# A state-space stage on one core: the loop of three turns of two groups becomes straight code on all five engines

## What is computed

```python
xz = einsum('bld,ed->ble', rmsnorm(layernorm(x)), in_proj_w); xi, z = split(xz, 2)
u = silu(conv4(xi) + conv_b)                      # 512 channels
dt, Bm, Cm = split(einsum('bld,ed->ble', u, x_proj_w))
delta = softplus(dt @ dt_proj_w.T + dt_proj_b)
def step(h, inp):                                 # one step for each of 1024 positions
    delta_t, B_t, C_t, u_t = inp
    h = exp(delta_t[..., None] * A) * h + (delta_t * u_t)[..., None] * B_t[:, None, :]
    return (h, einsum('bds,bs->bd', h, C_t))      # 16 states for each channel
y = (ys + u * D_param) * silu(z)
x = x + (x + y @ out_proj_w.T)                    # the block's input is layernorm(x)
```

## Time and profile before

| | |
|---|---|
| median of 3 runs | 3620.05 us (3619.46 to 3624.98) |
| the profiled execution's own time | 3639.42 us |
| its span, first to last instruction | 3637.7 us |
| this stage's scans, first to end (8 groups) | 65.1 to about 1030 us |
| the looped groups 1 to 6 | 184.6 to 914.6 us |
| busy over the span | PE 85%, DVE 68%, ACT 46%, POOL 44% |

### The profile page before, as it was taken

One profiled execution on the slowest core, in us unless ns is written; L12 is line 12 of the kernel. 1 busy time (PEld: TensorE's weight loads), 2 busy tenths in 40 slices (PEclk: granted clock), 3 DMA queues, 4 the chain that ended last, 5 costly groups with the idle time before them and its releaser, 6 DMA issues. The chain is left out here.

```text
span 3637.7 us, 53305 instructions
## 1 busy us (share of the span) xinstructions
PE 3093.1 (85%) x15700; PEld 1825.8 (50%) x15701; DVE 2460.9 (68%) x4639; ACT 1662.0 (46%) x3131; POOL 1618.1 (44%) x1645
## 2 busy tenths in 40 slices
PE   6898899889779799897988998976978787997795
PEld 3343334333258544445444486643654575664474
DVE  6999899999976585766858565973348672224245
ACT  5767666667445355574655653321223231223031
POOL 4998889889855312212131263115443000001643
PEclk9999999999999889898998999988999898998898
DMA  4555455556510000000000004501345791000246
GB/s 142 146 140 143 131 142 141 132 140 145 145 35 1 16 2 2 1 2 2 2 2 2 1 1 123 143 1 70 119 131 161 155 110 30 12 12 0 87 131 211
DMA packets 358189, 282.73 MB, mean 78 GB/s; under 512 B 214124, under 2 KB 274320, under 8 KB 357940
## 3 DMA queue, kind: packets, MB, share of 16 engines
q1 hardware_dynamic: 344884, 246.16, 26.8%
q0 software_dynamic: 13056, 33.65, 2.7%
HBM read 205.41 MB, written 76.16 MB: 77 GB/s over the span
## 5 line engine op out<-in xcount | busy, mean ns | idle before, releaser
L709 POOL TENSOR_TENSOR mamba_dBu<-mamba_du,mamba_bcs 128x512 f32<-128x512 f32 x512 | 639.5, 1272 | 95.4 <-DMA mamba_bcs<-mamba_bc 74.4
L628 PE MATMUL mamba_banks<-mamba_hc,ident 128*128 128x512 f32 x1024 | 529.7, 629 | 111.2 <-DVE mamba_hc L947 110.7
L873 ACT ACTIVATE mamba_banks<-mamba_delta,mamba_a_neg 128x512 f32<-128x512 f32 x512 | 351.9, 690 | 178.0 <-DVE mamba_hc L947 166.5
L1749 DVE TENSOR_REDUCE attn_mp<-attn_banks 128x1 f32<-128x512 f32 (+2 forms) x576 | 356.3, 679 | 49.5 <-PE attn_banks L1440 43.2
L628 PEld LDWEIGHTS mamba_banks<-mamba_hc,ident 128*128 128x128 f32 x1024 | 179.1, 194 | 418.2 <-DVE mamba_hc L947 302.6
L947 DVE TENSOR_TENSOR mamba_hc<-mamba_banks,mamba_bcs 128x512 f32<-128x512 f32 x512 | 343.1, 671 | 9.0 <-PE mamba_banks L628 9.0
L940 DVE TENSOR_TENSOR_SCAN mamba_banks<-mamba_banks,mamba_h_end,mamba_dBu 128x512 f32<-128x512 f32 x256 | 326.6, 1276 | 17.5 <-ACT mamba_banks L873 9.3
L940 DVE TENSOR_TENSOR_SCAN mamba_banks<-mamba_banks,mamba_dBu 128x512 f32<-128x512 f32 x256 | 312.1, 1219 | 36.1 <-POOL mamba_dBu L709 19.4
L1437 PE MATMUL attn_banks<-attn_kT,attn_qT 96*128 96x512 bf16 (+3 forms) x768 | 252.4, 363 | 9.5 <-ACT attn_kT L1631 5.3
L1451 PE MATMUL attn_banks<-attn_qT,attn_kT 98*128 98x512 bf16 (+3 forms) x768 | 210.2, 328 | 8.8 <-ACT attn_r L1649 4.0
L1116 POOL TENSOR_TENSOR ffn_hs<-ffn_h,ffn_hs 128x512 fp32r<-128x512 f32 x128 | 162.1, 1296 | 97.3 <-ACT ffn_hs L1145 97.3
(11 more groups left out here) (422 smaller groups left out, 6608.2 us busy)
## 6 DMA issues: line engine op xcount, KB each, us to landing
mamba_bcs<-mamba_bc SPq DMA_DIRECT2D x256, 512.0 KB, 5.0
moe_slots_moe<-moe_pad SPq DMA_DIRECT2D x2, 9252.0 KB, 53.2
moe_xg<-moe_slots_moe SPq DMA_DIRECT2D x144, 128.5 KB
mix_qkv<-mixA_qkv SPq DMA_DIRECT2D x8, 1536.0 KB, 5.9
mixA_y<-moe_rows SPq DMA_DIRECT2D x16, 512.0 KB, 6.0
mix_qk<-mix_qkv SPq DMA_DIRECT2D x16, 512.0 KB, 7.4
mix_v<-mix_qkv SPq DMA_DIRECT2D x16, 256.0 KB, 7.6
mix_out<-mixB_oh SPq DMA_DIRECT2D x16, 256.0 KB, 7.5
```

Source lines behind the costliest of these rows:

```text
L628: pe.matmul(banks[:, SUMS + k % PAIR, :], c.ident[:, :], hc[:, n % RING, :], start=False, stop=True, skip_group_check=True).then_inc(sem(" ...
L709: pool.tensor_tensor(dBu[:, n % RING, :], du[:, v, k, :], bcs[:, i_of(n) % 4, 0, :], ALU.mult)\
L873: act.activation(banks[:, n % RING, :], delta[:, v, k, :], ACT.Exp, scale=a_neg[:, k, st:st + 1])\
L1749: dve.tensor_reduce(dst, src, AX.X, ALU.max).then_inc(sem("ring_used"), 1)
```

## The change

```diff
--- before.py
+++ after.py
@@ -517,7 +517,7 @@
         def group_loop(engine, group):

             group(0, 0, False, True)
-            with engine.Fori(0, B - 1) as m:
+            for m in range(B - 1):
                 group(m * 2 + 1, 1, True, True)
                 group(m * 2 + 2, 0, True, True)
             group(G - 1, 1, True, False)
```

## The result

| | before | after |
|---|---|---|
| median of 5 runs | 3620.05 us (3614.08 to 3624.98) | 3596.57 us (3592.84 to 3600.58) |
| ratio | | 0.9939, 95% interval 0.9927 to 0.9951 |

The account below looks back on a forecast made before the run. The state-space stage was taken to run at DVE's pace, with fetch stalls at loop returns. Gains of 8.36 and 4.19 made 12.55 us, other terms zero, taking the 3620.05 median to 3607.5; range 3599 to 3615 (8 in 10).

Parts of the forecast that it names:

- The two returns on DVE: State-space loop: DVE's idle of 4.51 and 3.70 us at its two returns goes, worth 8.36 us by group lengths.
- Rival 2: State-space seams: stall only in the profiled execution, or POOL, ACT or a transfer late; gain 0 to 6 us, chance 0.12.
- What the stall leaves behind: Groups 3 and 5: PE's long idle, low clock and DVE's ninth-tile wait go, making them like group 1; 4.19 us.
- Rival 1: State-space stage: only the stall goes, the ninth tile's wait stays; gain 8.4 us, time 3611.7, chance 0.12.
- Sequencer arithmetic and the fetch of straight code: State-space stage: small loop instructions hidden by DVE's work, and fetching straight code hidden too; both costed at nothing.
- Rival 3: State-space groups on DVE: fetch of straight code isn't hidden, making the kernel slower; 3651 us, chance 0.05.
- What stands behind the stage: Later loops, attention's first: code moves, stalls stay but may change length; value 0, with 5 us either way.
- Rival 4: Attention's returns or a later loop get shorter by the move, 5 us and more on top; 3601, chance 0.08.
- The base: Whole kernel: the same 12.5 us come off the 3620.05 median as off the profiled 3639.42 us.

Follow-up runs that it names:

- e2: Kernel before with only DVE's state-space loop written straight, plus 45 semaphore increments holding DVE's later code in place: 3629.66 us, ratio 0.9969.
- e3: Kernel before with the state-space loop written straight on PE, ACT, POOL and SP, DVE keeping its loop: 3640.08 us, ratio 0.9991.
- the third measurement: The changed kernel, unaltered, timed a third time beside the kernel before on another chip: 3596.91 us, ratio 0.9952.
- e16: Kernel before with only DVE's state-space loop straight and 45 semaphore increments, repeated on a chip where before takes 3617.05: 3602.01 us, ratio 0.9962.
- e8: Changed kernel with attention's loop on DVE also written straight: 3624.55 us, ratio 0.9953 to before; the changed kernel took 3622.39 on that chip.

## Why the prediction came out as it did

**The two returns on DVE (8.36 us): right.** The idle ahead of the first scans is gone, e2 and e3 show that it was DVE's own code, and that POOL, which the trace names, was not what it waited for. Rival 2 fell with it: the stalls stood in every trace with DVE's loop, and the timed runs kept the gain.

**What the stall leaves behind (4.19 us): right.** PE's long idle, its stretch at the lower clock and the long wait at the ninth tile went together, and e3 shows them stay together. Groups 3 and 5 came out at 120.00 and 120.31, with 120.28 named. Rival 1 is refuted. The two terms are 12.55 us; the pair of traces has 13.2, all traces together 13.6, and the timed runs with DVE's part alone have 12.5. By a control-flow cost of 108 ns alone (the Trainium skill, Advanced Engine Details and Errata, section Control Flow Timing) this would have been next to nothing (0.2 us). The branch in the row does take 63 ns, and the time is behind it.

**Sequencer arithmetic and the fetch of straight code (0): right.** Busy times and group 7 are unchanged, and no "issue" wait appeared in the stage. Rival 3 fell for this reason.

**What stands behind the stage (value taken 0, 5 either way): here the prediction failed.** It named the place, attention's returns on DVE, and that the head's place in its packet decides. It then took zero, said that these stalls stay, and priced the gain that they might bring by how much longer they were than the first stage's second return (1.3 us for both), with 5 us either way beside it. What it missed is that such a wait comes in whole packets, as the experiments show. A wait of 4.2 us was two fetches, and the shift took one of them off each return, 2.3 and 2.5 us of waiting; the place of this code measured 4.6 us of the kernel's time on average instead of 0. The place of the head could have been counted in the built programs of before and after, 63 and 18 of 128, and the 8 KB of a packet stood in the earlier trace rows. Counting would not by itself have told which offset has the second fetch, but it would have shown that the offset changes by 45 of 128. With about 4.6 us for it the forecast would have been 3602.9, nearer to the result, which would still lie 6 us lower.

**The rest, 3 to 5 us.** 22.1 measured less 12.5 and 4.6 leaves 5; against the average of 20.6 over the three measurements it is 3.5. Of this 1.3 may be the other engines' code, which was costed at nothing. What remains isn't placed, and is within the scatter of one comparison. That the result fell 2.4 us below the range is therefore in part chance: a gain of 17.4 us, as the third measurement had, would have been 3602.7 here, inside it. Rival 4, "more than forecast", with 3601, was the case; its 0.08 was too low.

**The base.** That the same 12.5 us come off the median as off the slower profiled execution held: e2 and e16, on a chip where before takes 3641 us and on one where it takes 3617, have 11.3 and 13.7.

## What to carry to other kernels

A hardware loop can cost a fetch at each return: here DVE's loops of 756 and 529 instructions waited 1.8 to 5.1 us there, and the feed-forward's of 126 instructions went on within 0.3 us. On the engine that sets the pace the wait also leaves the others idle, and here PE's clock fell behind it; look for idle time ahead of the first instruction of a turn and compare it with the same passage where no return stands. In this stage only the engine that sets the pace needed its code straight: that one program brought 12.5 us, the other four together 1.3 on average, which can't be told from nothing. When an edit changes a program's length, list every loop behind it that waits at its return and work out where its head moves within a packet; and take two chips, and a repetition, before you believe a gain of 5 us in 3600.

## What was unexpected of the hardware

- DVE's code comes in packets of 8 KB that hold 128 instructions (39 packets for 4848 recorded instructions of four engines). Forty instructions of shift put the second wait between two particular statistics (1.53 and 1.68 us), 45 put it back ahead of the first instruction (4.40 and 4.46 in one), 128 changed nothing (4.29 and 4.24).
- The same wait costs unequally. Of 4.2 us at a return of attention, the first 2.3 us taken away brought about 2 us for each return on average, the remaining 2 us nothing that could be seen (e8, one batch).
- The chips differ: 3617 and 3620 us on some, 3641 to 3644 on others for the same program, with the difference in the two mixture blocks (about 12 us in each) and none seen in the state-space stage (the six groups, straight on DVE, last 716.8 to 720.5 us on the three chips that have such a trace).
